# Filter-tap arithmetic beside a feed-forward stage: from GpSimd to VectorE and ScalarE, and three memsets placed later

## The reference, cut to what matters

```python
dt = jnp.exp(log_dt)[:, None]
A = -jnp.exp(log_A_real) + 1j * A_imag
dtA = A * dt
C = (C_real + 1j * C_imag) * (jnp.exp(dtA) - 1.0) / A
K = 2.0 * jnp.einsum('dn,dnl->dl', C, jnp.exp(dtA[:, :, None] * t)).real
```

## Time and profile before

| | |
|---|---|
| time, median of 3 runs (lowest, highest) | 2641.59 us (2632.76, 2647.14) |
| the profiled execution: its own time, its span | 2636.16 us, 2634.2 us |
| busy share of the span: PE, DVE, ACT, POOL | 85%, 68%, 52%, 47% |
| mean granted TensorE clock | 0.959 |
| second feed-forward, first product to last aggregation | 1634.15 to 1858.98 us |

### The profile page before, as it was taken

One profiled execution on the slowest core, in us unless ns is written; L12 is line 12 of the kernel. 1 busy time (PEld: TensorE's weight loads), 2 busy tenths in 40 slices (PEclk: granted clock), 3 DMA queues, 4 the chain that ended last, 5 costly groups with the idle time before them and its releaser, 6 DMA issues. The chain is left out here.

```text
span 2634.2 us, 56043 instructions
## 1 busy us (share of the span) xinstructions
PE 2240.5 (85%) x20720; PEld 1615.4 (61%) x20720; DVE 1783.9 (68%) x4361; ACT 1376.2 (52%) x2116; POOL 1237.6 (47%) x1206
## 2 busy tenths in 40 slices
PE   7957777777899889899889987979798979999979
PEld 4535555555797555455555555868566846666658
DVE  6657777777767667767767764886454447767753
ACT  4532222222342488888878885433210457777753
POOL 4329999990101267656756752262464013223220
PEclk9979999999899799999999999989999989999999
DMA  5464545551101112111111111000000100000001
GB/s 181 140 183 134 145 143 143 166 140 45 49 1 36 46 57 63 51 47 61 60 57 52 58 42 36 1 1 1 15 0 0 39 0 1 1 1 1 1 1 65
DMA packets 158737, 149.06 MB, mean 57 GB/s; under 512 B 21440, under 2 KB 141376, under 8 KB 155392
## 3 DMA queue, kind: packets, MB, share of 16 engines
q1 hardware_dynamic: 138704, 105.51, 13.6%
q0 software_dynamic: 3456, 23.07, 2.6%
q10 hardware_dynamic: 16304, 16.83, 2.2%
HBM read 100.51 MB, written 40.63 MB: 54 GB/s over the span
## 5 line engine op out<-in xcount | busy, mean ns | idle before, releaser
L1761 POOL TENSOR_SCALAR a_dist<-a_dist,a_mq 128x512 f32<-128x512 f32 x512 | 358.1, 720 | 117.2 <-ACT a_mq L1700 117.2
L1804 DVE TENSOR_SCALAR_CACHE_REDUCE a_dist<-a_ring 128x512 f32<-128x512 f32 x512 | 332.1, 687 | 90.8 <-PE a_ring L1449 89.3
L1690 ACT ACTIVATE a_pT<-a_psT 128x1024 f32<-128x1024 f32 x256 | 258.3, 1025 | 94.5 <-PE a_psT L1461 87.1
L1461 PE MATMUL a_psT<-ident,a_dist 128*128 128x128 f32 x2048 | 266.6, 277 | 17.9 <-ACT a_pT L1690 17.7
L1461 PEld LDWEIGHTS a_psT<-ident,a_dist 128*128 128x128 f32 x2048 | 235.7, 143 | 49.9 <-issue 20.3
L1684 ACT ACTIVATE a_dist<-a_dist 128x2048 f32<-128x2048 f32 x128 | 237.2, 1903 | 41.5 <-DVE a_dist L1804 38.6
L1449 PE MATMUL a_ring<-a_stack 102*128 102x512 bf16 x512 | 183.8, 397 | 56.6 <-DVE a_dist L1804 32.9
L1449 PEld LDWEIGHTS a_ring<-a_stack 102*128 102x128 bf16 x512 | 47.5, 98 | 226.9 <-DVE a_dist L1804 161.5
L3283 ACT ACTIVATE ds_wtm<-ds_wg,ds_par 128x256 f32<-128x256 f32 x64 | 29.2, 503 | 269.1 <-DVE ds_wg L3413 264.7
L1474 PE MATMUL a_psO<-a_pT,a_va 128*32 128x512 f32 x1024 | 137.2, 612 | 2.3 <-ACT a_pT L1690 2.3
L2359 POOL TENSOR_TENSOR s_xdec<-s_xdt,s_dv 128x512 f32<-128x512 f32 x24 | 25.0, 1043 | 199.7 <-ACT s_dv L2288 189.9
(11 more groups left out here) (437 smaller groups left out, 6181.5 us busy)
## 6 DMA issues: line engine op xcount, KB each, us to landing
a_stack<-a_parts_dram SPq DMA_DIRECT2D x384, 64.0 KB
a_parts_dram<-a_parts SPq DMA_DIRECT2D x32, 384.0 KB, 2.5
bf_w<-in_up_w_dram POOLq DMA_DIRECT2D x10, 1024.0 KB
bf_w<-in_down_w_dram POOLq DMA_DIRECT2D x10, 1024.0 KB
ds_nbg<-tok_nbk ACTq DMA_DIRECT2D x128, 64.0 KB
feat_v<-di_part SPq DMA_DIRECT2D x16, 256.0 KB, 2.6
tok_nbk<-di_nbk SPq DMA_DIRECT2D x16, 256.0 KB, 3.0
feat_k<-di_part SPq DMA_DIRECT2D x16, 256.0 KB, 3.5
```

Source lines behind the costliest of these rows:

```text
L1461: last = turn(psT[:, u % 2, kb, q * P:(q + 1) * P], dist[:, g % 2, i, q, k * P:(k + 1) * P], core.ident[:])
L1690: a(pT[:, u // 2, u % 2], psT[:, u % 2], ACT.Exp).then_inc(exp_done, 1)
L1761: last = nc.gpsimd.tensor_scalar(d, d, -1.0, mq[:, g % 2, i, q:q + 1], ALU.mult, ALU.add)
L1804: ts(dist[:, gg % 2, i, q, :], ps[:], 1e-12, 3.0e38, ALU.max, ALU.min, accum_out=mq[:, gg % 2, i, q:q + 1]).then_inc(ring_out, 1)
```

## The change

1. The GpSimd queue of the taps is gone. Its wide steps go to VectorE, one piece at a time, at five places in a batch: before the first `add_rows` (j = 0) and after each of the four (j = 1 to 4, `after_rows`). Pieces are of 1024 elements per partition (a step of 2048 is cut into halves), except the rounding of `g`, which stays whole. The small steps move to such places too.
2. The 8 products with the channel mask go to ScalarE, four at the end of batch 5 and four at the end of batch 6 (`spread_taps`). ScalarE's other steps are called by b, with the rates' exponentials still at the end of batch 0, the other exponentials at the end of batch 1, the sines at the ends of batches 2 and 3. The sum and the sign change of `f_im` become one step.
3. The memsets at the start of the distance attention wait until the 8 hidden remainders of batch 0 of the first feed-forward are taken.
4. A form of the hidden block with two gelus, of which one writes the high part itself, for blocks m >= `TWICE`; `TWICE` is 8 and there are 8 blocks (m = 0 to 7), so no block takes it.

```diff
@@ FeedForward
+    TWICE = 8
...
+                gelu = lambda out: nc.scalar.activation(out, psH[m % 2], ACT.Gelu, bias=self.bf.bias_h[:, m:m + 1])
+                if m >= self.TWICE:
...
+                    gelu(self.h_hi[:, m, :])
+                gelu(self.h[:, n % self.RING, :]).then_inc(self.h_done, 1)
...
             for j in range(TPB):
                 add_rows(b, j)
+                after_rows(b, j)
@@ ffn_stage
-        @block.gpsimd
-        def _(pool):
-            beside.gpsimd(nc, pool)
...
-            ffn.vector(dve, lambda b, m: beside.vector(nc, dve, b, m))
+            ffn.vector(dve, lambda b, m: beside.vector(nc, dve, b, 0) if m == FeedForward.NH else None,
+                       lambda b, j: beside.vector(nc, dve, b, j + 1))
@@ ConvTaps
+    EXPS, DECAYS, ROOTS, POWERS, TAPS = 2, 5, 11, 14, 22
+    RATES, MAGS, PHASES, TURNS, SPREAD, READY = 7, 9, 12, 17, 48, 52
...
         if m == 0:
-            pe.wait_ge(self.wide, self.TAPS)
+            pe.wait_ge(self.vec, self.READY)
+            pe.wait_ge(self.act_n, self.TAPS)
...
+    def spread_taps(self, nc, act, q):
+        f = (self.f_re, self.f_im)[q]
+        to = self.fm[:, q].rearrange("p t (i c) -> p t i c", c=CPT)
+        for c in range(CPT):
+            nc.scalar.activation(to[:, :, :, c], f[:], ACT.Identity, scale=self.chan[:, c:c + 1]).then_inc(self.act_n, 1)
... scalar(b): b == 1 waits RATES, then MAGS; b == 2 PHASES; b == 3 TURNS
+        if b == 5:
+            act.wait_ge(self.vec, self.SPREAD)
+            self.spread_taps(nc, act, 1)
+        if b == 6:
+            act.wait_ge(self.vec, self.READY)
+            self.spread_taps(nc, act, 0)
... vector(b, j), the places (each step waits for its own semaphore)
+        if at == (0, 3):   # memset of half_pi and 5 small steps
+        if at == (0, 4):
+            step(tt(f3[1], over_i(DR), ix, ALU.mult))
+        if b == 1 and j < 2:
+            step(tt(g_mag[:, half(j)], over_j(DR, j), jx, ALU.mult))
+        if at == (1, 2):
+            step(tt(f3[0], over_i(TURN), ix, ALU.mult))
+        if at == (1, 3):
+            step(ts(f[:, 2, :], f[:, 0, :], ROUND, -ROUND, ALU.add, ALU.add))
+        if at == (1, 4):
+            step(tt(f[:, 0, :], f[:, 0, :], f[:, 2, :], ALU.subtract))
+        if b == 2 and j < 2:
+            step(tt(g_im[:, half(j)], over_j(TURN, j), jx, ALU.mult))
+        if at == (2, 2):
+            step(ts(g_re[:], g_im[:], ROUND, -ROUND, ALU.add, ALU.add))
+        if b == 2 and j > 2:
+            step(tt(g_im[:, half(j - 3)], g_im[:, half(j - 3)], g_re[:, half(j - 3)], ALU.subtract))
+        if at == (3, 0):
             dve.wait_ge(self.act_n, self.ROOTS)
+        if b == 3 and j < 2:
+            step(tt(f[:, 2 + j, :], f[:, 2 + j, :], f[:, 1, :], ALU.mult))
+        if at == (3, 2):   # 9 small steps
+        if at == (3, 3):   # 6 small steps, the last a reciprocal
+        if at == (3, 4):   # 8 small steps
+        if at == (4, 0) to (4, 4):   # one product, product, subtraction, product, product
+        if at == (5, 0):
+            step(stt(self.f_im[:], f3[0], -1.0, f3[1], ALU.mult, ALU.subtract))
+            dve.wait_ge(self.act_n, self.POWERS)
+        if b == 5 and j > 0:
+            g, u = (g_im, g_re)[(j - 1) // 2], half((j - 1) % 2)
+            step(tt(g[:, u], g[:, u], g_mag[:, u], ALU.mult))
@@ distance_attention_stage
         @block.gpsimd
         def _(pool):
+            pool.wait_ge(ffn.h_lo_done, FeedForward.NH)
             nc.gpsimd.memset(va[:], 0.0).then_inc(va_set, 1)
```

More of the change, by code:

```diff
@@ L396, in scalar, with vector @@
                 between(b)
-    def vector(self, dve, between):
+    def vector(self, dve, between, after_rows=lambda b, j: None):
         nc, core, bf, psT, psY, NH = self.nc, self.core, self.bf, self.psT, self.psY, self.NH
@@ L799, in __init__ @@
         self.steps = 0
-        self.wides = 0
     def allocate(self, core, ctx):
@@ L854, in scalar @@
             a(f[:, 3, :], f[:, 0, :], ACT.Abs).then_inc(self.act_n, 1)
-            act.wait_ge(self.act_n, 9)
+            act.wait_ge(self.act_n, self.ROOTS - 2)
             a(v[:, self.COS, :], v[:, self.ABS, :], ACT.Sin, scale=-2 * PI,
@@ L870, in vector @@
         tt, ts, stt = nc.vector.tensor_tensor, nc.vector.tensor_scalar, nc.vector.scalar_tensor_tensor
+        f3 = [f[:, q, :].rearrange("p (t i) -> p t i", i=NI) for q in range(4)]
+        over_i = lambda t: spread(t, [P, NMT, NI], 2)
+        ix = spread(idx[:, NJ:], [P, NMT, NI], 1)
+        HALF = NMT // 2
+        half = lambda u: slice(u * HALF, (u + 1) * HALF)
+        over_j = lambda t, u: spread(t[:, half(u)], [P, HALF, NJ], 2)
+        jx = spread(idx[:, 0:NJ], [P, HALF, NJ], 1)
         def step(ins):
@@ L916, in vector @@
             step(stt(NIM, T1, 2.0, DEN, ALU.mult, ALU.mult))
[L917 to L943, removed]
-        step(tt(g_im[:], g_im[:], g_re[:], ALU.subtract))
-        assert self.wides == self.PHASES
-        pool.wait_ge(self.act_n, self.ROOTS)
-        step(tt(f[:, 2, :], f[:, 2, :], f[:, 1, :], ALU.mult))
-        step(tt(f[:, 3, :], f[:, 3, :], f[:, 1, :], ALU.mult))
-        pool.wait_ge(self.act_n, self.POWERS)
-        step(tt(g_im[:], g_im[:], self.g_mag, ALU.mult))
-        step(tt(g_re[:], g_re[:], self.g_mag, ALU.mult))
-        pool.wait_ge(self.vec, self.MODES)
-        step(tt(f3[0], over_i(NRE), f3[3], ALU.mult))
-        step(tt(f3[1], over_i(NIM), f3[2], ALU.mult))
-        step(tt(self.f_re[:], f3[0], f3[1], ALU.subtract))
-        step(tt(f3[0], over_i(NRE), f3[2], ALU.mult))
-        step(tt(f3[1], over_i(NIM), f3[3], ALU.mult))
-        step(tt(self.f_im[:], f3[0], f3[1], ALU.add))
-        step(ts(self.f_im[:], self.f_im[:], -1.0, None, ALU.mult))
-        assert self.wides == self.SPREAD
-        for q in range(2):
-            for c in range(CPT):
-                dst = self.fm[:, q].rearrange("p t (i c) -> p t i c", c=CPT)[:, :, :, c]
-                step(ts(dst, (self.f_re, self.f_im)[q][:], self.chan[:, c:c + 1], None, ALU.mult))
-        assert self.wides == self.TAPS
@@ new lines, in vector @@
+        if at == (4, 0):
+            step(tt(f3[0], over_i(NRE), f3[3], ALU.mult))
+        if at == (4, 1):
+            step(tt(f3[1], over_i(NIM), f3[2], ALU.mult))
+        if at == (4, 2):
+            step(tt(self.f_re[:], f3[0], f3[1], ALU.subtract))
+        if at == (4, 3):
+            step(tt(f3[0], over_i(NRE), f3[2], ALU.mult))
+        if at == (4, 4):
+            step(tt(f3[1], over_i(NIM), f3[3], ALU.mult))
+        if at == (5, 0):
+            step(stt(self.f_im[:], f3[0], -1.0, f3[1], ALU.mult, ALU.subtract))
+            assert self.steps == self.SPREAD
+            dve.wait_ge(self.act_n, self.POWERS)
@@ L968, in conv_spectra @@
+        if b == 5 and j > 0:
+            g, u = (g_im, g_re)[(j - 1) // 2], half((j - 1) % 2)
+            step(tt(g[:, u], g[:, u], g_mag[:, u], ALU.mult))
+        if at == (5, 4):
+            assert self.steps == self.READY
 def conv_spectra(nc, core, lc, ck, scales_tag):
```

50 lines of the change are left out of this document (23 added, 27 removed).

## The result

The changed kernel takes 2605.86 us (median of 4 runs, 2602.1 to 2614.63), the kernel before beside it 2639.49 (2632.76 to 2647.14). The ratio is 0.9876, with 0.9838 to 0.9915 as its 95% interval: 33.6 us less, between 22.4 and 42.8. The forecast was 2602.

A forecast was written before the change was run, and what follows sets the result against it. TensorE, held up in the second feed-forward because GpSimd keeps VectorE out of SBUF, was taken as the bound; 31.2 + 7.8 = 39.0 us off the profiled 2636.16 gives 2597.2, as a median 2602, range 2590 to 2616.

The forecast's parts named there:

- the two terms: Second feed-forward without GpSimd's taps, 31.2 us off; first feed-forward's weight casts no longer beside memsets, 7.8 us off.
- the ring of 4: Second feed-forward's hidden blocks: the ring lets VectorE be about 4 us late before TensorE waits.
- The pieces: VectorE's new tap steps in the second feed-forward: about 1.23 us each, also with spread operands; far bound 2.45.
- Rival C: Second feed-forward: pieces with spread operands take 2.45 us, TensorE waits some 2 us a batch; 2612 us, chance 0.09.
- The walk: Second feed-forward, VectorE tile by tile: batches 0, 1, 2, 5 at most 0.6 us late, batch 3 3.3; TensorE loses 0.
- the far bound: ScalarE's four mask products at the end of batches 5 and 6: 9.1 us if stride 4 doubles their 4.6.
- the visit: ScalarE's tap work at the end of a second feed-forward batch: 11.9 us of room before the next gelu.
- the margin: Second feed-forward: the next gelu, queued behind ScalarE's waits, has 3 us to spare; added cost 0.
- Rival B: First feed-forward, batch 0: the large memset keeps out a bias addition, 5 us more; 2607 us, chance 0.10.
- The single row: Kernel before: a subtraction with two SBUF inputs kept its normal 1.22 us beside the large memset; so cost 0.
- D: Second feed-forward: VectorE's lag makes TensorE wait some 3 us a batch and its clock falls; 2671 us, chance 0.03.
- E: Second feed-forward: TensorE's waits are not due to GpSimd, only the memsets' 7.8 us come; 2634 us, chance 0.03.

The follow-up runs named there:

- experiment 1: Each half alone: the changed kernel with early memsets, ratio 0.9872 to the kernel before; the kernel before with only the memsets made to wait, 0.9968.
- Experiment 3: The changed kernel with one more product of 1024 elements at each of the five places of batches 1 to 5; second feed-forward 219.32 us against 193.62.
- Experiment 7: The changed kernel with ScalarE's mask products flat with scale in the real half, strided without scale in the imaginary half; second feed-forward 193.75 us.
- experiment 5: The changed kernel with six GpSimd memsets in each of batches 1 to 5; second feed-forward 194.87 us beside the additions, 210.25 us beside the casts.
- experiment 4: The changed kernel with the eight mask products back on GpSimd, each as one `tensor_scalar`; second feed-forward 201.08 us, 7.5 more.
- experiment 2: The changed kernel with all pieces of a batch at one place, ahead of its first tile; second feed-forward 224.70 us.

## Why the prediction was right

**The sum.** 31.2 and 7.8 were forecast, 31.21 and 7.75 came. The reading behind it (batch 6 shows the pace that is left when GpSimd is quiet) gave the stage within 0.1 us, and experiment 1 shows that the two terms add. That the whole time is only 3.9 us above the forecast is in part luck, since the runs of one kernel lie 12 to 14 us apart in the result and up to 27 in experiment 1; in the profiled pair the difference, 10.80, is the stretch of unchanged code.

**The waits.** One reading was short. The prediction names `h_lo`, 8.2 us, as what TensorE waits for. Its largest wait was another one; the view by waits of the kernel before, batches 1 to 6, TensorE and ScalarE:

```profile
PE f_psH L327 <- ACT f_h L390: 10.7, 3, 4.5
PE f_psY L343 <- DVE f_h_lo L428: 8.2, 6, 2.5
ACT f_h L390 <- DVE f_h_lo L428: 20.2, 6, 5.3
```

The gelus for which TensorE waited 10.7 us were themselves waiting for `h_lo`, through the ring of 4, so the cause is the same. With 1.6 us for `X` TensorE idled 20.55 us; the other 11.74 of the 32.29 us are longer products, 149.09 us busy instead of 137.35.

**The pieces.** 1.21 us measured, 1.25 with its wait reckoned. Rival C (2.45) is refuted. Experiment 3 doesn't price it: the rival would have lengthened 9 pieces in batches 1, 2 and 4, and the experiment adds one at all 25 places.

**The walk.** Its additions of batch 2 come 2.57, 2.58 and 2.57 us apart (1700.74, 1703.31, 1705.89, 1708.46), as the 2.58 of the chain said. Batch 3, the additions at 1723.82, 1726.39, 1730.02 and 1733.16, and its end:

```profile
1736.03 0.38 DVE L472 BATCH_NORM_AGGREGATE mv<-bn 128x2 f32<-128x6 f32 x4
1736.32 0.40 DVE L433 CAST f_h_hi<-f_h 128x512 fp32r<-128x512 f32 x1
```

With the old batch 0 and then 23.08 a batch, aggregation would end at 1637.10 + 26.24 + 3 x 23.08 = 1732.58, and the first cast start 0.80 later; it starts 2.9 late, 3.3 were reckoned. The walk lists five additions for batch 3, which has four; the last, 11.9, belongs to none. The ring takes the delay: TensorE has no idle time in batches 1 to 6. Batches 0, 1 and 2 end 1.07, 1.07 and 1.39 us behind that pace, so 0.3, 0.3 and 0.6 behind the next block's due time, as the walk had it.

**ScalarE.** The waits for `MAGS` and `SPREAD` are there (2.62 and 2.58 us idle), and end before the next gelu is due. The mask products were the term that was mis-sized, 1.98 us each (7.92 for four) against 1.14; the far bound, 9.1, held. The wait for `SPREAD` was not reckoned at all: with it the visit at the end of batch 5 has 10.5 of the 11.9 us. In order of time, at the end of batch 5:

```profile
1769.45 7.92 ACT L845 ACTIVATE ck_fm<-ck_f_im,ck_chan 128x1024 f32<-128x1024 f32 x4 [2.58 <-DVE ck_f_im L974]
1778.76 0.69 ACT L392 ACTIVATE f_h<-f_psH,bf_bias_h 128x512 f32<-128x512 f32 x1 [1.38 <-PE f_psH L331]
```

The next gelu still waits 1.38 us for TensorE, so some cover was left, less than the 3 us that I named as the margin. Experiment 7 names the cause, the stride.

**The memsets.** Rival B is refuted: the bias addition beside the long memset takes 0.41 us. The single row on which this rested was right, and experiment 5 has operations with two SBUF inputs at 0.42 and 1.21 us beside memsets throughout. The rule weighed against it, from the Trainium skill, GPSIMD Engine Reference, Key points, is too wide here. The Trainium skill, SBUF — State Buffer, section "Who interferes with whom", has it narrower: a VectorE instruction with two SBUF inputs contends with a GpSimd instruction that reads SBUF, not with one that only writes it, while a cast in a two-port mode contends with both. The rows agree on who is held up: GpSimd's two-operand steps and its `tensor_scalar`, which read, held up both kinds (3.84 us in the earlier trace rows, 1.48 in experiment 4), and memsets, which only write, the casts and the rounding alone. They don't agree on how long: by that section the second to issue is blocked until the other ends, but beside the `tensor_scalar` of 4.1 us every second cast and subtraction of experiment 4 kept 0.41 and 0.69.

**Rivals D and E.** Batches 1 to 6 of after have clock 1.00 (batch 0 has 0.94, as before), so D did not occur. That it isn't empty, experiment 2 shows: with the same pieces in one place TensorE waits 21.4 us and has 0.93 of its clock, and the whole gain of the stage is gone. What kept the change from it are the places, which the walk went through tile by tile. E is refuted by 31.21 us.

## What to carry to other kernels

A GpSimd instruction can cost VectorE nearly its whole duration, however little it computes (a cast took 3.87 us beside a product of 3.98): look for instructions of one engine that end just after instructions of the other. Moving the work off GpSimd paid here because each piece is shorter than the gap that it is put into; walk the gaps one by one, since the same work in one place gave nothing. To judge a change of 1%, cut the spans at marks that both kernels have, and compare the stretches.

## What the runs showed of the hardware

- A memset on GpSimd holds up VectorE's casts and its one-operand rounding; the two beside a memset of 6.92 us took 6.62 and 6.89 us and ended 0.6 and 0.3 us after it, and the rounding took 2.37 instead of 1.23. It does not hold up the products, subtractions and additions with two operands in SBUF (1.21, 0.69, 0.42), nor the statistics (0.43). GpSimd's steps with two operands hold up both the casts and the additions (3.87 beside a product of 3.98, 3.84 beside a subtraction of 4.67). A run of `tensor_scalar` steps of 4.1 us holds up every second cast by 1.1 us and the subtraction behind it by 0.8.
- GpSimd's memset takes 0.88 ns an element for 2296 float32 in each of 128 partitions, and 0.84 for 8192 bfloat16 in each of 32.
- ScalarE writes 1024 float32 a partition with a stride of 4 elements in 1.9 to 2.0 us, and flat in 1.1.
- Unchanged code at the start of the kernel, with much DMA traffic, took 650.07 to 667.91 us, with a granted clock of 0.83 to 1.00 from 80 to 120 us; what decides it was not found.
